# Switched attention: small matrix products in three groups per tile in place of six, routing later in the round

## The chip, the cores and the metric

One core of one Trainium2 chip. The core has five engines that run in parallel and meet at semaphores: TensorE (PE, with its weight loads as PEld), VectorE (DVE), ScalarE (ACT), GpSimd (POOL) and SyncE (SP, which here starts the transfers). The metric is the time of one execution on the device, in microseconds (us).

## The reference, cut to what matters

The whole is a model of four layers on x of 128 sequences x 64 positions x 128 features. Each layer adds a cross attention and a feed-forward part to x. The change touches the last part alone, the "switched attention" of layer 3:

```python
def _get_sel_gate(x, w, route_scale):              # per position and head: best 2 of 8 experts
    probs = jax.nn.sigmoid((x @ w.T).reshape(B, S, H, E))
    vals, idx = jax.lax.top_k(probs, K)
    vals = vals / jnp.clip(vals.sum(-1, keepdims=True), 1e-09) * route_scale
    return (jax.nn.one_hot(idx, E) * vals[..., None]).sum(-2)
...
x = layernorm(x)                                   # H = 8 heads, E = 8 experts, P = 128, K = 2
q = jnp.einsum('bsd,hpd->bhsp', x, q_w.reshape(H, P, D))
k = jnp.einsum('bsd,hpd->bhsp', x, k_w.reshape(H, P, D))
v = jnp.einsum('bshep,bshe->bhsp', jnp.einsum('bsd,hedp->bshep', x, v_w), gate_v)
att = jax.nn.softmax(jnp.einsum('bhqp,bhkp->bhqk', q, k) * P ** -0.5, axis=-1)
ctx = jnp.einsum('bhqk,bhkp->bqhp', att, v)
out = jnp.einsum('bshep,hepd->bsd', ctx[:, :, :, None, :] * gate_o[..., None], o_w)
```

All 64 experts are computed for every position, and the gates (zero for six of eight) weight their outputs. The result is added to the part's input, with the factor tanh(g_ffn[3]).

## The kernel before, in words

`program` runs the layers one after the other. The last two calls are the cross attention of layer 3, which leaves x in a scratch buffer in memory, and `switch_attention` (from L1687), which writes the output. Its helper `prepare_switch` (L1603) loads and splits the expert weights into a high and a low part, and keeps two small weights: `pair` (the product of query and key weights of each head, so that scores are x·pair·x) and `sel` (the routing weights of both gates).

**Tiles and rounds.** A tile is 128 rows of x (two sequences); there are 64. `straight` (L36) writes the program out: for every round t it goes through a list of stages (lag, step) and emits step for tile t - lag. Each engine has such a list of its own, and its order is the order of the code; semaphores tie them together. In round t the engines work on the v half of tile t - 2, the o half of tile t - 3, and the preparation of tile t - 1.

**Units.** The big work is 16 units a round, v0 to v7 (values of head 0 to 7) and o0 to o7 (outputs). A unit is six matmuls with 512 columns (L2062): three (high x high, high x low, low x high) into an accumulator bank `ps_a` for four experts, then three into a bank `ps_d` for the other four. There are two banks of each kind, used in turn, so bank d of a unit waits until the unit two before it has been read. ScalarE reads bank a (`scale`, L1850: four scalings by the gates), VectorE reads bank d (`mix`, L1964: four operations, each a gated product added to a partial sum, in two halves h0 and h1 of two). GpSimd adds the scaled parts: `add_v` (L1789, L1794) makes the values v, `add_o` (L1806 to L1816) and `finish` (L1823 to L1829) the output.

**Small products of TensorE, per round:** `turn_x` (L2070) transposes the normalised tile; `turns[0]` and `turns[1]` (L2077) transpose the softmax numerators; `logits` (L2082) is the routing product; `pair_keys(0)` and `(1)` (L2091) multiply by `pair`; `scores` (L2115); `context` (L2104) multiplies probabilities by v. Before the change these stand in six groups among the units: turn_x with turns[0] after v1; turns[1] with logits after v2; pair_keys(0) after v4; pair_keys(1) after v5; scores after o0; context after o1.

**VectorE's order.** The table `between` says what stands behind each half of each mix. `norm` (L244) is the first stage of the round: it normalises the tile that turn_x then transposes. `sums` (L1930 to L1934) makes gate_o. `route(n)` are the 20 steps of the top-2 routing of the next tile (L1973 to L1994), each waiting for the one before; step 0 waits for ScalarE's exponential of the logits, and step 19 writes gate_v, for which v0 of the next round waits on ScalarE and on VectorE. `peak` (L2016) takes the row maximum of the scores and `shifts` (L2022) scales and negates it; the exponentials of ScalarE use it as their bias. `low_ctx(b)` (L2010) makes the low part of the context. `front(n)` are the first three steps of the layer norm of a tile one round ahead (L217 to L223); GpSimd's `rstd` (L236), which stands between o5 and o6 in its list, needs front(2) and is needed by `norm`.

**ScalarE's order.** Scalings in unit order; keep_x (L1860, L1861) after v1, exp_logits (L1873) and keep_probs (L1867) after v3, keep_u after v5 and v6, keep_ctx and the exponentials (L1899) in the o half.

```python
def straight(stages, bufs=2, tiles=TILES):
    for t in range(tiles + max(lag for lag, _ in stages)):
        for lag, step in stages:
            if 0 <= t - lag < tiles:
                step(t - lag, (t - lag) % bufs, (t - lag) // bufs)
```

Of the kernel before, what the change touches and what calls it, by code (L numbers as in the profile page):

```python
# [1602 lines left out]
def prepare_switch(k, A, C):  # L1603
# [9 lines left out]
    with k.scope():  # L1613
# [8 lines left out]
        with nc.Block() as block:  # L1622
# [30 lines left out]
            @block.vector  # L1653
            def _(dve):
                dve.wait_ge(q["pair_ps"], 1)
                for n in range(2):
                    dve.tensor_copy(W["pair"][:, 4 * n:4 * n + 4], ps[n]).then_inc(q["kept"], 1)
                dve.wait_ge(q["sel_ps"], 1)
                dve.tensor_copy(W["sel"][:], ps_sel).then_inc(q["kept"], 1)
                ones = C["ones"][:, 0:SH]  # L1660
                dve.tensor_scalar(W["route"][:, 0], ones, rs[:], None, ALU.mult).then_inc(q["kept"], 1)
                dve.tensor_scalar(W["route"][:, 1], ones, rs[:], C["gates"][:, 7:8], ALU.mult, ALU.mult)\
                    .then_inc(q["kept"], 1)
                for h in range(SH):
                    for m, n in enumerate(("v", "o")):
                        dve.wait_ge(q["high"], 2 * h + m + 1)
                        dve.tensor_tensor(W[n]["low"][:, h], staged[:, h % 3, m], W[n]["high"][:, h].bitcast(F32),
                                          ALU.subtract)\
                            .then_inc(q["low"], 1)
# [17 lines left out]
def switch_attention(k, A, C, x_in, out):  # L1687
# [6 lines left out]
    with k.scope():  # L1694
# [9 lines left out]
        top = k.sb("sw_top", [P, SH])  # L1704
# [31 lines left out]
                   "ranked", "u", "uT", "scores", "top", "shift", "exp", "p_turned", "p_kept", "rsum",  # L1736
# [10 lines left out]
        with nc.Block() as block:  # L1747
# [87 lines left out]
            def _(act):  # L1835
# [58 lines left out]
                def exp_scores(i, s, rd, lo):  # L1894
                    act.wait_ge(q["shift"], i + 1)
                    if lo == 0 and not first(i, 2):
                        act.wait_ge(q["p_turned"], 2 * (i - 1))
                    for h in range(lo, lo + 2):
                        act.activation(probs[:, s, h], ps_s[:, h], ACT.Exp, bias=shift[:, s, h:h + 1],  # L1899
                                       scale=float(P) ** -0.5, accum_out=total[:, s, h:h + 1]).then_inc(q["exp"], 1)  # L1900
                exps = [(1, lambda i, s, rd, lo=lo: exp_scores(i, s, rd, lo)) for lo in range(0, SH, 2)]
                vs, os = ([(lag, scale(kind, h)) for h in range(SH)] for kind, lag in (("v", 2), ("o", 3)))
                stages = vs[:2] + [(1, keep_x)] + vs[2:4] + [(1, exp_logits), (2, keep_probs)] + vs[4:6]
# [5 lines left out]
            def _(dve):  # L1909
# [104 lines left out]
                def peak(i, s, rd):  # L2014
                    dve.wait_ge(q["scores"], i + 1)
                    dve.tensor_reduce(top[:], ps_s, AX.X, ALU.max).then_inc(q["top"], 1)  # L2016

                def shifts(i, s, rd):
                    dve.wait_ge(q["top"], i + 1)
                    if not first(i, 2):  # L2020
                        dve.wait_ge(q["exp"], SH * (i - 1))
                    dve.tensor_scalar(shift[:, s], top[:], -float(P) ** -0.5, None, ALU.mult).then_inc(q["shift"], 1)  # L2022

                mixes = {(kind, h): [(lag, mix(kind, h, half)) for half in range(2)]
                         for kind, lag in (("v", 2), ("o", 3)) for h in range(SH)}
# [3 lines left out]
                    "v": [[], [], [(2, sums(0))], [(2, sums(1))], [(2, sums(2))], [], *R[0:5], R[5] + R[6], R[7],  # L2029
                          R[8] + R[9], R[10], R[11]],  # L2030
                    "o": [R[12], R[13] + R[14], R[15] + R[16], [(1, peak)], [(1, shifts)], R[17], R[18],
                          [(2, low_ctx(0))], [(0, front(0))], R[19] + [(0, front(1))], [(0, front(2))],
                          [(2, low_ctx(1))], [], [], [], []],
# [8 lines left out]
            def _(pe):  # L2042
# [76 lines left out]
                stages = vs[:2] + [(1, turn_x), turns[0], vs[2], turns[1], (1, logits), vs[3], vs[4], (1, pair_keys(0))]  # L2119
                stages += [vs[5], (1, pair_keys(1)), vs[6], vs[7], os[0], (1, scores), os[1], (2, context)]  # L2120
# [52 lines left out]
```

## Time and profile before

| what | us |
|---|---|
| time, median of 3 runs | 3384.04 (3339.35 to 3385.38) |
| the profiled execution | 3386.34, its span 3384.6 |
| PE busy | 3020.6 (89%) |
| DVE busy | 2829.0 (84%) |
| ACT busy | 2356.9 (70%) |
| POOL busy | 2325.1 (69%) |
| first expert unit of the switched attention on TensorE | starts at 1467.54 |

The profile is of one execution. Each row of an engine's timeline has the start from the span's beginning, the duration, the engine, the line of the code, the operation, out<-in by the program's names, shapes, and xN where N equal ones in a row are merged (the duration then is from the first start to the last end). Operations of one engine overlap a little, since the next starts before the end of the one before is recorded; matmuls do so most, so for them the distance of two starts is the cost, not the duration. What stands in brackets is the engine's idle time before the row and who ended it. The view by stretches has the stretch, its length, then for PE, PEld, DVE, ACT and POOL the busy us and (xinstructions), the granted clock of TensorE (1.00 is full), the share of the DMA engines and GB/s.

### The profile page before, as it was taken

Reading aid. Unit: us, or ns where it says so; the run is one execution under the profiler, and the core shown is the slowest. Engines: PE = TensorE matmul, PEld = TensorE weight load, DVE = VectorE, ACT = ScalarE, POOL = GpSimd, SP = SyncE. Lnnn points to the kernel's source line nnn. Section 1 sums busy time; section 2 is a strip of 40 time slices with the busy share of each in tenths; the row PEclk is TensorE's granted clock in tenths of the full one; section 3 lists DMA queues with packets and bytes.
Section 4 is the critical chain, followed back from the end, with each engine's and each line's share of the span. In section 5 each row is a group of like instructions: output and inputs, shape, how many; then the busy total and the mean of one; then the engine's idle time right before and its main releaser. Section 6 shows DMA issues by size and latency. Waiting matters only on the chain.

```text
span 3384.6 us, 79947 instructions
## 1 busy us (share of the span) xinstructions
PE 3020.6 (89%) x24889; PEld 2212.5 (65%) x24902; DVE 2829.0 (84%) x9292; ACT 2356.9 (70%) x7581; POOL 2325.1 (69%) x3156
## 2 busy tenths in 40 slices
PE   6944999549865999679999999999999999999998
PEld 3522777427543677557777777777777777777776
DVE  4455999669897899678998899998899898889887
ACT  2345666678697666557777777777777777777776
POOL 1236999556487666237777777777777777777777
PEclk9999999759876999879999999999999999999999
DMA  1101000012100011310000000000000000000000
GB/s 53 55 8 18 16 16 16 3 40 79 43 1 7 27 31 30 89 48 9 8 8 8 7 8 8 9 8 8 7 8 8 8 9 7 9 7 8 9 8 5
DMA packets 134373, 63.81 MB, mean 19 GB/s; under 512 B 21824, under 2 KB 133568, under 8 KB 133952
## 3 DMA queue, kind: packets, MB, share of 16 engines
q1 hardware_dynamic: 133952, 58.70, 6.3%
q8 instruction: 202, 3.31, 0.4%
q14 instruction: 219, 1.79, 0.2%
HBM read 41.81 MB, written 8.45 MB: 15 GB/s over the span
## 4 chain that ended last, share of the span: by engine, by line
PE 56%; POOL 0%; DVE 0%; ACT 0%; issue 0%; DMA 0%; POOLq 0%; SPq 0%; DVEq 0%; ACTq 0%
PE ps_sw_a L2062 23%; PE ps_sw_d L2062 21%; PE ps_sw_w L2104 4%; PE ps_sw_w L2091 3%; PE ps_sw_s L2077 2%; PE ps_sw_s L2115 2%; PE ps_sw_m L2082 1%; PE ps_sw_m L2070 0%; ACT sw_scaled L1850 0%; DVE sw_v_part L1964 0%; POOL sw_o_rest L1813 0%; POOL sw_o_rest L1816 0%; DMA sw_x<-scratch_x 0%; POOL sw_o_rest L1809 0%; POOL sw_o_pair L1825 0%
## 5 line engine op out<-in xcount | busy, mean ns | idle before, releaser
L1850 ACT ACTIVATE sw_scaled<-ps_sw_a,sw_gate_o 128x128 f32<-128x128 f32 x2048 | 620.3, 447 | 252.3 <-PE ps_sw_a L2062 244.2
L1850 ACT ACTIVATE sw_scaled<-ps_sw_a,sw_gate_v 128x128 f32<-128x128 f32 x2048 | 597.4, 450 | 203.3 <-PE ps_sw_a L2062 203.2
L1964 DVE SCALAR_TENSOR_TENSOR sw_o_part<-ps_sw_d,sw_gate_o,sw_o_part 128x128 f32<-128x128 f32 x1920 | 554.7, 337 | 60.4 <-PE ps_sw_d L2062 59.4
L1789 POOL TENSOR_TENSOR sw_v_pair<-sw_v_part,sw_scaled 128x256 f32<-128x256 f32 x512 | 377.9, 738 | 159.1 <-DVE sw_v_part L1964 105.5
L1964 DVE SCALAR_TENSOR_TENSOR sw_v_part<-ps_sw_d,sw_gate_v,sw_scaled 128x128 f32<-128x128 f32 x1024 | 304.6, 338 | 124.2 <-PE ps_sw_d L2062 102.7
L1813 POOL TENSOR_TENSOR sw_o_rest<-sw_o_rest,sw_scaled 128x256 f32<-128x256 f32 x384 | 285.2, 743 | 154.6 <-ACT sw_scaled L1850 117.3
L1964 DVE SCALAR_TENSOR_TENSOR sw_v_part<-ps_sw_d,sw_gate_v,sw_v_part 128x128 f32<-128x128 f32 x1024 | 304.3, 338 | 0.0
L1816 POOL TENSOR_TENSOR sw_o_rest<-sw_o_rest,sw_scaled 128x256 f32<-128x256 f32 x384 | 282.6, 736 | 30.1
L1794 POOL TENSOR_TENSOR sw_v<-sw_v_pair 128x128 f32<-128x128 f32 x512 | 241.6, 472 | 40.2
L920 POOL TENSOR_TENSOR at_key_wide<-at_keyT,c_half_heads 128x1024 f32<-128x1024 f32 x128 | 242.5, 1895 | 4.2 <-ACT at_keyT L1017 4.2
L2062 PE MATMUL ps_sw_a<-sw_v_high,sw_xT_high 128*128 128x512 f32 x512 | 235.8, 461 | 0.0
L2062 PE MATMUL ps_sw_a<-sw_o_high,sw_ctx_high 128*128 128x512 f32 x512 | 214.7, 419 | 0.6 <-ACT sw_scaled L1850 0.6
L2062 PE MATMUL ps_sw_d<-sw_v_high,sw_xT_high 128*128 128x512 f32 x512 | 208.2, 407 | 0.0
L2062 PE MATMUL ps_sw_d<-sw_o_high,sw_ctx_high 128*128 128x512 f32 x512 | 207.1, 404 | 0.0
L2062 PE MATMUL ps_sw_d<-sw_v_low,sw_xT_high 128*128 128x512 f32 x512 | 203.2, 397 | 0.0
L2062 PE MATMUL ps_sw_a<-sw_v_low,sw_xT_high 128*128 128x512 f32 x512 | 202.9, 396 | 0.0
L2062 PE MATMUL ps_sw_a<-sw_v_high,sw_xT_low 128*128 128x512 f32 x512 | 202.5, 395 | 0.0
L2062 PE MATMUL ps_sw_a<-sw_o_low,sw_ctx_high 128*128 128x512 f32 x512 | 202.0, 395 | 0.0
L2062 PE MATMUL ps_sw_d<-sw_v_high,sw_xT_low 128*128 128x512 f32 x512 | 202.0, 395 | 0.0
L2062 PE MATMUL ps_sw_d<-sw_o_low,sw_ctx_high 128*128 128x512 f32 x512 | 201.4, 393 | 0.0
L2062 PE MATMUL ps_sw_a<-sw_o_high,sw_ctx_low 128*128 128x512 f32 x512 | 200.4, 391 | 0.0
L2062 PE MATMUL ps_sw_d<-sw_o_high,sw_ctx_low 128*128 128x512 f32 x512 | 200.4, 391 | 0.0
(318 smaller groups left out, 8768.4 us busy)
## 6 DMA issues: line engine op xcount, KB each, us to landing
at_ctxT<-ctx_T SPq DMA_DIRECT2D x128, 64.0 KB, 1.8
re_values<-in_ctx SPq DMA_DIRECT2D x128, 64.0 KB, 2.3
x<-in_x SPq DMA_DIRECT2D x64, 64.0 KB, 1.8
l_ctx<-in_ctx SPq DMA_DIRECT2D x64, 64.0 KB, 2.0
re_ctx<-in_ctx SPq DMA_DIRECT2D x16, 256.0 KB, 3.3
scratch_x<-x SPq DMA_DIRECT2D x64, 64.0 KB, 1.8
swp_staged<-in_L_ffn_v_w SPq DMA_DIRECT2D x8, 512.0 KB, 5.6
swp_staged<-in_L_ffn_o_w SPq DMA_DIRECT2D x8, 512.0 KB, 6.9
```

Source lines behind the costliest of these rows:

```text
L920: pool.tensor_tensor(key_wide[:, s], keyT[:, s].unsqueeze(1).broadcast_to([P, HALF, P]), C["half_heads"][:].unsqueeze(2).broadcast_to([P, ...
L1789: pool.tensor_tensor(v_pair[:, h % 2], v_part[:, h], scaled[:, h % 4, 2:4], ALU.add)\
L1794: pool.tensor_tensor(v[:, h], v_pair[:, h % 2, 0], v_pair[:, h % 2, 1], ALU.add).then_inc(q["v"], 1)
L1813: pool.tensor_tensor(o_rest[:, 0:2], o_rest[:, 0:2], scaled[:, h % 4, 0:2], ALU.add)\
L1816: pool.tensor_tensor(o_rest[:, 2:4], o_rest[:, 2:4], scaled[:, h % 4, 2:4], ALU.add)\
L1850: act.activation(scaled[:, h % 4, e], ps_a[h % 2][:, e], ACT.Copy, scale=gates[:, s, h, HALF_E + e:HALF_E + e + 1]).then_inc(a_scaled[kind ...
L1964: dve.scalar_tensor_tensor(out=acc[:, e % 2], in0=ps_d[h % 2][:, e], scalar=gates[:, s, h, e:e + 1], in1=before, op0=ALU.mult, op1=ALU.add ...
L2062: m = pe.matmul(bank, lhs[a], w[b][:, h, experts], start=c == 0, stop=c == 2)
L2077: m = pe.matmul(ps_s[t, h], probs[t, s, h], C["ident"][t, t], start=True, stop=True)
L2091: m = pe.matmul(ps_w[n][:, h * P:(h + 1) * P], W["pair"][:, 4 * n + h], xT[:, s], start=True, stop=True)
L2104: m = pe.matmul(ps_w[b][:, h * S:(h + 1) * S], v[t, h], probs_T[t, h], start=True, stop=True)
L2115: m = pe.matmul(ps_s[t], xT[:, s, t], uT[:, :, t], start=True, stop=True)
```

## The change

TensorE's small products stand in three groups: turn_x with both turns after v1; logits with both pair_keys after v4; scores with context after o1. VectorE's routing starts after the first half of v5 (before: of v3) and its 20 steps run to the end of the round; peak stands behind the first half of o2 (before: the second half of o1); front(0) to front(2) stand between o4 and o6. ScalarE's keep_probs stands behind v2 and its exp_logits behind v4. The factor P ** -0.5 goes into the weights `pair`, so that the scores come scaled; the reduction of peak writes its result negated, and shifts, its buffer and its semaphore are gone.

```diff
@@ prepare_switch, VectorE @@
                 for n in range(2):
-                    dve.tensor_copy(W["pair"][:, 4 * n:4 * n + 4], ps[n]).then_inc(q["kept"], 1)
+                    dve.tensor_scalar(W["pair"][:, 4 * n:4 * n + 4], ps[n], float(P) ** -0.5, None, ALU.mult).then_inc(q["kept"], 1)
@@ switch_attention @@
-        top = k.sb("sw_top", [P, SH])
         shift = k.sb("sw_shift", [P, 2, SH])
...
-                   "ranked", "u", "uT", "scores", "top", "shift", "exp", "p_turned", "p_kept", "rsum",
+                   "ranked", "u", "uT", "scores", "shift", "exp", "p_turned", "p_kept", "rsum",
@@ ScalarE @@
                         act.activation(probs[:, s, h], ps_s[:, h], ACT.Exp, bias=shift[:, s, h:h + 1],
-                                       scale=float(P) ** -0.5, accum_out=total[:, s, h:h + 1]).then_inc(q["exp"], 1)
+                                       accum_out=total[:, s, h:h + 1]).then_inc(q["exp"], 1)
...
-                stages = vs[:2] + [(1, keep_x)] + vs[2:4] + [(1, exp_logits), (2, keep_probs)] + vs[4:6]
+                stages = vs[:2] + [(1, keep_x), vs[2], (2, keep_probs)] + vs[3:5] + [(1, exp_logits), vs[5]]
@@ VectorE @@
                 def peak(i, s, rd):
                     dve.wait_ge(q["scores"], i + 1)
-                    dve.tensor_reduce(top[:], ps_s, AX.X, ALU.max).then_inc(q["top"], 1)
-
-                def shifts(i, s, rd):
-                    dve.wait_ge(q["top"], i + 1)
                     if not first(i, 2):
                         dve.wait_ge(q["exp"], SH * (i - 1))
-                    dve.tensor_scalar(shift[:, s], top[:], -float(P) ** -0.5, None, ALU.mult).then_inc(q["shift"], 1)
+                    dve.tensor_reduce(shift[:, s], ps_s, AX.X, ALU.max, negate=True).then_inc(q["shift"], 1)
...
-                    "v": [[], [], [(2, sums(0))], [(2, sums(1))], [(2, sums(2))], [], *R[0:5], R[5] + R[6], R[7],
-                          R[8] + R[9], R[10], R[11]],
-                    "o": [R[12], R[13] + R[14], R[15] + R[16], [(1, peak)], [(1, shifts)], R[17], R[18],
-                          [(2, low_ctx(0))], [(0, front(0))], R[19] + [(0, front(1))], [(0, front(2))],
-                          [(2, low_ctx(1))], [], [], [], []],
+                    "v": [[], [], [(2, sums(0))], [(2, sums(1))], [(2, sums(2))], [], [], [], [], [], R[0], R[1], R[2], R[3],
+                          R[4], R[5]],
+                    "o": [R[6], R[7], R[8], R[9], [(1, peak)], R[10] + R[11], R[12], [(2, low_ctx(0))], R[13],
+                          R[14] + [(0, front(0))], R[15] + [(0, front(1))], [(2, low_ctx(1))], R[16] + [(0, front(2))],
+                          R[17], R[18], R[19]],
@@ TensorE @@
-                stages = vs[:2] + [(1, turn_x), turns[0], vs[2], turns[1], (1, logits), vs[3], vs[4], (1, pair_keys(0))]
-                stages += [vs[5], (1, pair_keys(1)), vs[6], vs[7], os[0], (1, scores), os[1], (2, context)]
+                stages = vs[:2] + [(1, turn_x)] + turns + vs[2:5] + [(1, logits), (1, pair_keys(0)), (1, pair_keys(1))]
+                stages += vs[5:] + os[:2] + [(1, scores), (2, context)]
                 stages += os[2:]
```

## Rows read from the trace of the kernel before

**Rows 1.** The view by stretches, 600 us of the steady stage (columns: see above)

```profile
2300.00:2900.00 600.00, 600.00 (x3702) 456.99 (x3702) 540.25 (x1914) 455.15 (x1774) 457.57 (x709) 1.00 0.03 8
```

**Rows 2.** VectorE in order of time, one round: start us, us, engine, what [idle before]

```profile
2502.87 2.14 DVE L1964 SCALAR_TENSOR_TENSOR sw_o_part<-ps_sw_d,sw_gate_o,sw_o_part 128x128 f32<-128x128 f32 x8
2504.94 0.79 DVE L244 TENSOR_SCALAR sw_xhat<-sw_x,sw_mv,sw_rstd 128x128 f32<-128x128 f32 x1
...
2508.87 0.61 DVE L1964 SCALAR_TENSOR_TENSOR sw_v_part<-ps_sw_d,sw_gate_v,sw_scaled 128x128 f32<-128x128 f32 x2 [0.60 <-PE ps_sw_d L2062]
...
2511.30 0.61 DVE L1964 SCALAR_TENSOR_TENSOR sw_v_part<-ps_sw_d,sw_gate_v,sw_scaled 128x128 f32<-128x128 f32 x2 [0.88 <-PE ps_sw_d L2062]
...
2514.31 0.59 DVE L1964 SCALAR_TENSOR_TENSOR sw_v_part<-ps_sw_d,sw_gate_v,sw_v_part 128x128 f32<-128x128 f32 x2
...
2520.18 0.28 DVE L1984 TENSOR_TENSOR sw_r_w<-sw_r_eq,sw_place 128x128 f32<-128x128 f32 x1
...
2524.61 0.68 DVE L2016 TENSOR_REDUCE sw_top<-ps_sw_s 128x8 f32<-128x512 f32 x1
2526.16 0.61 DVE L1964 SCALAR_TENSOR_TENSOR sw_o_part<-ps_sw_d,sw_gate_o,sw_o_part 128x128 f32<-128x128 f32 x2 [0.87 <-PE ps_sw_d L2062]
2526.68 0.16 DVE L2022 TENSOR_SCALAR sw_shift<-sw_top 128x8 f32<-128x8 f32 x1
...
2534.70 0.79 DVE L244 TENSOR_SCALAR sw_xhat<-sw_x,sw_mv,sw_rstd 128x128 f32<-128x128 f32 x1
```

**Rows 3.** TensorE in order of time, the same round

```profile
2506.33 0.27 PE L2070 MATMUL ps_sw_m<-c_ident,sw_xhat 128*128 128x128 f32 x1
...
2508.41 0.40 PE L2062 MATMUL ps_sw_d<-sw_v_high,sw_xT_low 128*128 128x512 f32 x1
2508.74 0.68 PE L2077 MATMUL ps_sw_s<-c_ident,sw_probs 64*64 64x64 f32 x16
...
2509.60 0.48 PE L2062 MATMUL ps_sw_a<-sw_v_high,sw_xT_high 128*128 128x512 f32 x1
2509.92 0.39 PE L2062 MATMUL ps_sw_a<-sw_v_low,sw_xT_high 128*128 128x512 f32 x1
...
2512.25 0.40 PE L2062 MATMUL ps_sw_d<-sw_v_high,sw_xT_low 128*128 128x512 f32 x1
2512.48 1.05 PE L2091 MATMUL ps_sw_w<-sw_xT,sw_pair 128*128 128x128 f32 x8
...
2515.58 0.48 PE L2062 MATMUL ps_sw_a<-sw_v_high,sw_xT_high 128*128 128x512 f32 x1
...
2519.15 0.39 PE L2062 MATMUL ps_sw_d<-sw_o_high,sw_ctx_high 128*128 128x512 f32 x1
...
2519.61 0.39 PE L2062 MATMUL ps_sw_d<-sw_o_high,sw_ctx_low 128*128 128x512 f32 x1
2519.93 1.08 PE L2115 MATMUL ps_sw_s<-sw_uT,sw_xT 128*64 128x512 f32 x4
...
2522.53 2.00 PE L2104 MATMUL ps_sw_w<-sw_probs_T,sw_v 64*128 64x64 f32 x32
```

**Rows 4.** ScalarE and GpSimd in order of time, the same round

```profile
2508.15 1.14 ACT L1850 ACTIVATE sw_scaled<-ps_sw_a,sw_gate_v 128x128 f32<-128x128 f32 x4 [0.39 <-PE ps_sw_a L2062]
...
2516.59 0.74 POOL L1789 TENSOR_TENSOR sw_v_pair<-sw_v_part,sw_scaled 128x256 f32<-128x256 f32 x1 [0.27 <-DVE sw_v_part L1964]
...
2521.94 0.46 POOL L1794 TENSOR_TENSOR sw_v<-sw_v_pair 128x128 f32<-128x128 f32 x1
```

**Rows 5.** All engines in order of time, the first round

```profile
1459.33 0.35 DVE L244 TENSOR_SCALAR sw_xhat<-sw_x,sw_mv,sw_rstd 128x128 f32<-128x128 f32 x1 [0.66 <-POOL sw_rstd L236]
...
1459.73 0.47 PE L2070 MATMUL ps_sw_m<-c_ident,sw_xhat 128*128 128x128 f32 x1 [33.63 <-DVE sw_xhat L244]
```

**Rows 6.** The tile sw_r_sel: how often, ns shortest/median/longest, first and last start

```profile
L1979 DVE TENSOR_TENSOR sw_r_sel<-sw_r_w,sw_m_w x54: 797/806/812, 1713.6 to 3289.4; 128x128 f32<-128x128 f32 x54
...
L1986 DVE TENSOR_TENSOR sw_r_sel<-sw_r_w,sw_m_w x54: 386/401/406, 1718.6 to 3294.4; 128x128 f32<-128x128 f32 x54
```

## The prediction

> **What bounds the kernel now.** I read the page's slices first: from about 1,460 us to the end the kernel is in the switched attention, TensorE near full in each slice. The view by stretches makes it exact [rows 1]: in 600 us of the steady stage TensorE is busy for all 600, VectorE for 540, ScalarE for 455, GpSimd for 458, at a granted clock of 1.00 (the 2.4 GHz level). So TensorE sets the pace and VectorE, at 90%, is the next. Two normalised tiles, one round apart, start at 2504.94 and 2534.70 on VectorE [rows 2]: a round is 29.76 us, and there are 64 tiles.
>
> Second, TensorE in order of time [rows 3]. A matmul of a unit (six with 512 columns, bank a and then bank d) starts 0.23 us after the one before (2519.15 to 2519.61 are two steps). Around the small products it is longer. After a group, the first matmul of the unit holds its successor back for 0.32 (2509.60 to 2509.92): 0.09 for leaving a group. Entering costs 0.10 ahead of the turned probabilities (2508.41 to 2508.74 is 0.33 against 0.23), 0.09 ahead of the scores (2519.61 to 2519.93), and nothing ahead of the paired keys (2512.25 to 2512.48). That is the whole gain to be had from fewer groups.
>
> Third, VectorE in the same round [rows 2]. It waits for TensorE at v2 (0.60), v3 (0.88) and o2 (0.87); from o2 at 2526.16 it runs without a gap until it starts the next tile's normalisation at 2534.70. TensorE needs the result of that for its first small product, turn_x. So there is a second loop beside TensorE's own: turn_x at 2506.33 [rows 3], TensorE's work up to VectorE's start on o2 (19.83 us), VectorE's unbroken stretch (8.54), the normalisation (0.79). That is 29.16 of the 29.76 us. The loop through VectorE has 0.60 us to spare, and this is the number on which the change turns.
>
> **The change part by part.** *Grouping.* The three exits that go are worth 3 x 0.09 = 0.27; the entry of the second turn_probs goes too, 0.10. Logits now enter from a unit, 128x128 as the paired keys are, so at nothing. Context now follows scores: I give 0 of its 0.09 entry back, since its tile shape (64*128) differs from that of the scores (128*64), and keep 0.09 as the upper end. Sum 0.37 us per round, bounds 0.27 to 0.46. Lengths of the products stay.
>
> On that 0.09 the Trainium skill speaks, in TensorEngine Tiling (Array Packing), Key Properties: changing the tiling mode drains TensorE. The rows agree in that only the groups that begin with 64-row or 64-column tiles pay to enter [rows 3]; by the rule scores to context pays on, and without it a round would be 0.09 shorter.
>
> *VectorE's order.* The work sum hardly changes: shifts goes (0.16 us busy, about 0.08 of its time as the next starts 0.08 before its end), negating in the reduction I take at nothing (bounds 0 and the 0.08 it saves) [rows 2]. What changes is where it stands. Routing starts after v5 in place of v3, because the logits now come behind v4. Before, steps 10 to 16 and the peak stood ahead of o2: from step 10 at 2520.18 to the start of the peak at 2524.61, plus its 0.60 (0.68 less the 0.08), is 5.03 us [rows 2]. In it stand ten mixes of 0.26 (eight run 2.14 with a last overlap of 0.08, so 2.06/8), 2.60. The rest, 2.43, is now behind the gate of o2. Less the 0.08 of shifts, the unbroken stretch grows by 2.35 us: 8.54 to 10.89. Nothing in the stretch goes elsewhere; step 17 to 19, both low_ctx and the three front steps were in it already. The time freed lies ahead of v5 and is idle there: VectorE is done with v4 before v5 is made, and with routing not begun it has nothing to do.
>
> *A new wait at o0.* Bank d of o0 needs the mixes of v6. VectorE's chain v5, step 0, v5, step 1, v6, step 2, v6 is as long as v3 to v4 was: 2511.30 to 2514.31 and 0.60 for the last pair, 3.61 us, and it starts 0.46 behind v5's last matmul (as 2508.41 and 2508.87 show for v2): done at 4.07. TensorE, with both paired keys already behind it, wants the bank 0.23 + (2519.15 - 2515.58 - 0.09) = 3.71 us after that matmul [rows 2, 3]. It waits 0.36, with the signal 0.38; bounds 0 and 0.5 (o1 has the same with v7, nearly hidden). Queued behind it are o0, o1, scores and context, and so the gate of o2.
>
> *Context and GpSimd.* Context stood at 2522.53, 0.13 behind the end of GpSimd's last v sum at 2522.40 [rows 3, 4]. Its TensorE time moves up by 0.37, which the 0.38 at o0 returns, so I take 0; bounds 0 and 0.2.
>
> *Handover to turn_x.* It was hidden: its weights were loaded under the unit before. Now TensorE waits for the normalisation, as in the first round, where it took 0.05 from 1459.68 (1459.33 and 0.35) to the start, and the transpose had 0.47 in place of 0.27 [rows 5]. I take 0.25, bounds 0.05 and 0.3. Also queued behind the normalisation: the gates of step 19, for which ScalarE's first v scaling waits. Step 19 ends 0.79 + 0.25 ahead of turn_x's start and four scalings take 1.14 [rows 4], so v0's bank is free 0.1 into the small products, and v2 asks for it only behind turn_x and both turn_probs: covered.
>
> *The port of VectorE and GpSimd.* The same comparison takes 0.81 at one place (L1979) and 0.40 at another (L1986), over 54 rounds each [rows 6]. At 2516.59 GpSimd had just begun a sum of 0.74 [rows 4], between v5 and v6 where the slow one stands. Normalising takes 0.79, against 0.35 in the first round, when GpSimd was idle. Moving routing among GpSimd's o sums can add such waits (up to +0.5 for steps 10 and 12 to 15), and GpSimd's new wait for front(2), now after o6, can take some away (xhat at 0.35: -0.44). I take 0.
>
> In the skill, SBUF — State Buffer, Who interferes with whom, says that an instruction of VectorE with two SBUF inputs is blocked by a GpSimd one that reads SBUF until that ends. By that rule steps 10 to 14 all stand at risk in the o half, and the round would be up to the 0.5 longer that I keep as an end.
>
> *Rest.* ScalarE's keep_probs moves ahead of the logits' exponential; both have several us before their readers. ScalarE has 24% idle [rows 1]. The scaled pair weights are two instructions in the preparation. GpSimd's o6 and o7 come later by its wait for front(2), but stay about as far from turn_x. SP's transfers keep their waits. All at 0.
>
> **Sum.** Loop after: (19.83 - 0.37) + 0.38 + 10.89 + 0.79 + 0.25 = 31.77 us, against 29.76: +2.01 us per round. Handovers with an o half before them: 61 of the 64. 61 x 2.01 = +123 us. The profiled execution took 3386.34 (span 3384.6), 2.3 above the median of 3384.04; 3384 + 123 = 3507 us.
>
> **Rivals.** (1) *The VectorE loop does not bind*, the round stays TensorE's: -0.37 x 64 = -24, so 3360 us, not slower. For it: the gain itself is in the rows. Against: it needs a VectorE loop under 29.39, 2.4 us less than I add up; it decides from a stretch after o2 of 8.5 us, and 2.35 us of work were put there. Chance 0.13. A faster result over 2% (under 3316) would need a gain of over 1 us per round, which no row offers: 0.04.
> (2) *Half as bad*: normalising unblocked (-0.44), no wait at o0 (-0.38), handover 0.05 (-0.2): +1.0 per round, 3445 us, within 2%. For it: GpSimd then stands still while it waits for front(2). Chance 0.11.
> (3) *Worse*: port waits +0.5 and o0, o1 and context at their upper ends (+0.3): 2.01 + 0.8 = +2.8 per round, 3384 + 61 x 2.8 = 3555 us. For it: GpSimd is busy in 76% of the time [rows 1]. Against: the eight mixes of the row at 2502.87 keep their 0.26 each all the same [rows 2], so only the routing steps are open to it. Chance 0.14.
> My forecast has the remaining 0.58.
>
> **Numbers.** 2% is 68 us, about what a measurement of this kernel can tell from no change, or 1.1 us per round. Slower 0.78 (forecast, rival 3 and about half of rival 2), same 0.18, faster 0.04. The range runs from rival 2's side, 3435, to 3565; rival 1 and a little are left out.
>
> **What would show it.** The profile after should have: a round of 31.8 us between two normalisations; VectorE never waiting for TensorE between o2 and the normalisation, that stretch near 10.9; TensorE idle or with late starts at bank d of o6, o7, v0, v1, and at turn_x, released by VectorE (some 2.4 us per round); VectorE idle over 2 us ahead of v5; three exits from small groups per round. If turn_x does not wait for the normalisation, the forecast is wrong at its root. If it does and the round is not 31 to 32.5, a term (port, o0, handover) is mis-sized.

## Result and the profile after

The changed kernel takes 3456.86 us (median of 6 runs, 3454.93 to 3457.21) against 3384.68 (6 runs). The ratio is 1.0249 with a 95% interval of 1.0191 to 1.0307: slower by 72 us, where 123 were predicted. That it is slower is clear; whether by more than 2% is not, since the interval reaches below. The profiled execution spans 3455.2 us. One thing is needed to read the medians and intervals: single executions of some versions, two of the six of the kernel before among them (3339.35 and 3340.9), are 43 to 51 us shorter, and in the one profile of such an execution (the first experiment below) the difference lies ahead of the switched attention, whose first normalised tile stands at 1411.1 us there and at 1461.2 in the changed kernel.

The stretches of the steady stage first (columns as in rows 1), of the changed kernel:

```profile
2300.00:2900.00 600.00, 587.74 (x3548) 437.60 (x3547) 489.46 (x1826) 441.67 (x1706) 448.54 (x685) 1.00 0.03 8
```

TensorE is no longer busy throughout, and VectorE fell further, from 540 to 489 us of 600. No engine is full: the time is in a chain that goes back and forth between two of them. VectorE in order of time, one round of the changed kernel:

```profile
2522.31 0.61 DVE L1963 SCALAR_TENSOR_TENSOR sw_v_part<-ps_sw_d,sw_gate_v,sw_scaled 128x128 f32<-128x128 f32 x2 [2.28 <-PE ps_sw_d L2057]
...
2532.72 0.61 DVE L1963 SCALAR_TENSOR_TENSOR sw_o_part<-ps_sw_d,sw_gate_o,sw_o_part 128x128 f32<-128x128 f32 x2 [2.23 <-PE ps_sw_d L2057]
2533.24 0.68 DVE L2017 TENSOR_REDUCE sw_shift<-ps_sw_s 128x8 f32<-128x512 f32 x1
...
2541.11 0.60 DVE L1963 SCALAR_TENSOR_TENSOR sw_o_part<-ps_sw_d,sw_gate_o,sw_o_part 128x128 f32<-128x128 f32 x2
...
2543.34 0.34 DVE L244 TENSOR_SCALAR sw_xhat<-sw_x,sw_mv,sw_rstd 128x128 f32<-128x128 f32 x1
...
2553.19 0.61 DVE L1963 SCALAR_TENSOR_TENSOR sw_v_part<-ps_sw_d,sw_gate_v,sw_scaled 128x128 f32<-128x128 f32 x2 [2.28 <-PE ps_sw_d L2057]
```

From v5 (2522.31) to the next v5 (2553.19) the round is 30.88 us; before, it was 29.76 [rows 2]. VectorE stands idle for 2.28 us ahead of v5 and for 2.23 ahead of o2, where it had 0.87, and then runs from o2 to the normalisation in 10.62 us (2532.72 to 2543.34), where it took 8.54. 61 rounds x 1.12 = 68 of the 72 us. The reduction that now negates (2533.24) takes 0.68 as the plain one did.

TensorE in the same round, around bank d of o0, o5 and v0, and at turn_x:

```profile
2525.35 0.40 PE L2057 MATMUL ps_sw_a<-sw_o_high,sw_ctx_low 128*128 128x512 f32 x1
2525.62 0.50 PE L2057 MATMUL ps_sw_d<-sw_o_high,sw_ctx_high 128*128 128x512 f32 x1
2525.96 0.40 PE L2057 MATMUL ps_sw_d<-sw_o_low,sw_ctx_high 128*128 128x512 f32 x1
...
2535.79 0.39 PE L2057 MATMUL ps_sw_a<-sw_o_high,sw_ctx_low 128*128 128x512 f32 x1
2536.56 0.51 PE L2057 MATMUL ps_sw_d<-sw_o_high,sw_ctx_high 128*128 128x512 f32 x1 [0.38 <-DVE sw_o_part L1963]
...
2541.26 0.40 PE L2057 MATMUL ps_sw_a<-sw_v_high,sw_xT_low 128*128 128x512 f32 x1
2541.76 0.51 PE L2057 MATMUL ps_sw_d<-sw_v_high,sw_xT_high 128*128 128x512 f32 x1
...
2543.74 0.39 PE L2057 MATMUL ps_sw_d<-sw_v_high,sw_xT_low 128*128 128x512 f32 x1
2543.97 0.27 PE L2065 MATMUL ps_sw_m<-c_ident,sw_xhat 128*128 128x128 f32 x1
```

A step of 0.23 is free of waits. At bank d of o5 it is 0.77 (2535.79 to 2536.56), of o6 0.56, of o7 0.33, of v0 0.50; of o0 0.27 and of o1 0.29, and a first matmul behind such a wait holds its successor back for 0.34 (2525.62 to 2525.96), so 0.11 more. Turn_x does not wait: 2543.74 to 2543.97 is 0.23, and the normalisation had ended at 2543.68. The waits view of 1,700 to 3,300 us (us in total, times, longest) names both sides of the chain, and a third party:

```profile
PEld ps_sw_d L2057 <- DVE sw_o_part L1963: 127.3, 250, 0.8
DVE sw_o_part L1963 <- PE ps_sw_d L2057: 113.8, 51, 2.3
POOL sw_rstd L236 <- DVE sw_var L223: 60.4, 52, 1.2
```

### The profile page after: what moved, and what is told of

It is laid out like the page before. It is cut to its first block, busy times and chain, and to the rows that moved or that the text cites. A ratio compares the mean times of both kernels' runs of the same rounds, so it can differ in the third digit from the quotient of the medians.

```text
span 3455.2 us, 79883 instructions
## 1 busy us (share of the span) xinstructions
PE 3046.0 (88%) x24889; PEld 2200.7 (64%) x24902; DVE 2730.4 (79%) x9228; ACT 2368.7 (69%) x7581; POOL 2347.9 (68%) x3156
## 4 chain that ended last, share of the span: by engine, by line
PE 40%; DVE 15%; issue 2%; POOL 0%; ACT 0%; DMA 0%; POOLq 0%; SPq 0%; DVEq 0%; ACTq 0%
PE ps_sw_d L2057 15%; PE ps_sw_a L2057 14%; DVE sw_o_part L1963 8%; PE ps_sw_w L2099 4%; PE ps_sw_w L2086 3%; DVE sw_ctx_low L2009 2%; PE ps_sw_s L2072 2%; PE ps_sw_s L2110 2%; DVE sw_shift L2017 1%; DVE sw_r_w L1983 1%; DVE sw_chosen L1987 1%; PE ps_sw_m L2077 0%; DVE sw_stats L217 0%; DVE sw_r_sel L1986 0%; DVE sw_r_sel L1985 0%
## 5 line engine op out<-in xcount | busy, mean ns | idle before, releaser
L1849 ACT ACTIVATE sw_scaled<-ps_sw_a,sw_gate_o 128x128 f32<-128x128 f32 x2048 | 602.5, 406 | 255.9 <-PE ps_sw_a L2057 250.8
L1849 ACT ACTIVATE sw_scaled<-ps_sw_a,sw_gate_v 128x128 f32<-128x128 f32 x2048 | 586.8, 393 | 261.1 <-PE ps_sw_a L2057 251.7
L1963 DVE SCALAR_TENSOR_TENSOR sw_o_part<-ps_sw_d,sw_gate_o,sw_o_part 128x128 f32<-128x128 f32 x1920 | 568.4, 338 | 145.0 <-PE ps_sw_d L2057 144.9
L1812 POOL TENSOR_TENSOR sw_o_rest<-sw_o_rest,sw_scaled 128x256 f32<-128x256 f32 x384 | 286.5, 746 | 219.8 <-ACT sw_scaled L1849 182.5
L1815 POOL TENSOR_TENSOR sw_o_rest<-sw_o_rest,sw_scaled 128x256 f32<-128x256 f32 x384 | 296.2, 771 | 30.1
L2057 PE MATMUL ps_sw_d<-sw_o_high,sw_ctx_high 128*128 128x512 f32 x512 | 234.7, 458 | 33.5 <-DVE sw_o_part L1963 33.3
L2057 PE MATMUL ps_sw_a<-sw_v_high,sw_xT_high 128*128 128x512 f32 x512 | 215.3, 420 | 0.0
```

The costliest lines, as they stand in the source:

```text
L1812: pool.tensor_tensor(o_rest[:, 0:2], o_rest[:, 0:2], scaled[:, h % 4, 0:2], ALU.add)\
L1815: pool.tensor_tensor(o_rest[:, 2:4], o_rest[:, 2:4], scaled[:, h % 4, 2:4], ALU.add)\
L1849: act.activation(scaled[:, h % 4, e], ps_a[h % 2][:, e], ACT.Copy, scale=gates[:, s, h, HALF_E + e:HALF_E + e + 1]).then_inc(a_scaled[kind ...
L1963: dve.scalar_tensor_tensor(out=acc[:, e % 2], in0=ps_d[h % 2][:, e], scalar=gates[:, s, h, e:e + 1], in1=before, op0=ALU.mult, op1=ALU.add ...
L2057: m = pe.matmul(bank, lhs[a], w[b][:, h, experts], start=c == 0, stop=c == 2)
```

## Experiments

Theory: a loop through VectorE sets the round, made of TensorE's work from turn_x to o2 and VectorE's unbroken stretch from o2 on. Rivals: the new groups on TensorE cost the time; VectorE's total work does; another engine takes over.

### The groups undone, the late routing kept

```diff
-                stages = vs[:2] + [(1, turn_x)] + turns + vs[2:5] + [(1, logits), (1, pair_keys(0)), (1, pair_keys(1))]
-                stages += vs[5:] + os[:2] + [(1, scores), (2, context)]
+                stages = vs[:2] + [(1, turn_x), turns[0], vs[2], turns[1], (1, logits), vs[3], vs[4], (1, pair_keys(0))]
+                stages += [vs[5], (1, pair_keys(1)), vs[6], vs[7], os[0], (1, scores), os[1], (2, context)]
```

ScalarE's list went back to the order before as well.

> The changed kernel, with TensorE's and ScalarE's lists as they were before (six groups); VectorE's late routing stays. Theory (the loop through VectorE sets the round: TensorE from turn_x to o2, then VectorE's unbroken stretch): the stretch stays at 10.6 us, TensorE's part is 0.37 longer for the grouping and 0.3 shorter since it need not wait at o0 and o1, so the round stays at 30.9 to 31.1 us and the time at 3455 to 3470 us. Rival (the new groups on TensorE cost the time, for instance since ScalarE and VectorE get their inputs in bunches): it goes back to 3384 us or near it.

Measured: four executions, 3423.25, 3426.89, 3470.0 and 3471.06 us, median 3448.45, ratio 1.0177 (1.0112 to 1.0242). The first two have the head start described above, so it is the other two that stand against the changed kernel's 3457: 13 to 14 us longer, at the upper end of what was expected. The rounds of its profile settle the matter. Two normalised tiles in a row, VectorE:

```profile
2503.36 0.34 DVE L244 TENSOR_SCALAR sw_xhat<-sw_x,sw_mv,sw_rstd 128x128 f32<-128x128 f32 x1
...
2534.48 0.34 DVE L244 TENSOR_SCALAR sw_xhat<-sw_x,sw_mv,sw_rstd 128x128 f32<-128x128 f32 x1
```

A round of 31.12 us, 0.24 longer than with three groups. The groups are not what costs; they save a little, and late routing costs by itself. The 0.24 is what the later experiments leave to expect: 0.55 for the grouping, less the 0.32 for the late starts at o0 and o1, which are absent here.

### Part of the routing back ahead of o2

The three groups stay. Steps 10 to 12, or 10 to 16, are put behind o1, in VectorE's idle time ahead of o2:

```diff
-                    "o": [R[6], R[7], R[8], R[9], [(1, peak)], R[10] + R[11], R[12], ...
+                    "o": [R[6], R[7], R[8], R[9] + R[10] + R[11] + R[12], [(1, peak)], [], [], ...
```

> The changed kernel with only steps 10 to 12 put ahead of the wait for o2. They take 1.03 us of the stretch. Theory (each us taken from the stretch is a us of the round until TensorE's own loop binds): 62 x 1.0 us less, 3395 us, a round of 29.9 us. Rival (another engine takes over at once, so that there is no slope of one): a gain of under half of that, 3425 us or more.

> The changed kernel with routing steps 10 to 16 put behind o1, ahead of the wait for o2; all groups stay three. In the changed profile these steps take 1.6 us of the stretch behind o2, and VectorE stands idle for 2.23 us ahead of o2. Theory: they disappear into the idle time, the loop through VectorE falls to 29.25 us, TensorE's own loop of 29.4 to 29.7 takes over, and the time is 3360 to 3382 us: not over the kernel before. Rival (groups cost the time): it stays at 3457 us. Rival (VectorE's total work bounds): stays within 10 us of 3457.

Measured: 3394.64 us (3393.27 to 3394.99) with steps 10 to 12, and 3376.64 (3375.01 to 3377.74, ratio to the kernel before 0.9967, 0.9952 to 0.9982) with 10 to 16. Both fell where they were expected. The first is a slope of one: 1.03 us taken from the stretch, 62 us off the time. VectorE of the version with steps 10 to 12, from one normalised tile to the next:

```profile
2508.22 0.34 DVE L244 TENSOR_SCALAR sw_xhat<-sw_x,sw_mv,sw_rstd 128x128 f32<-128x128 f32 x1
...
2528.46 0.61 DVE L1963 SCALAR_TENSOR_TENSOR sw_o_part<-ps_sw_d,sw_gate_o,sw_o_part 128x128 f32<-128x128 f32 x2 [1.27 <-PE ps_sw_d L2057]
...
2538.07 0.34 DVE L244 TENSOR_SCALAR sw_xhat<-sw_x,sw_mv,sw_rstd 128x128 f32<-128x128 f32 x1
```

The round is 29.85 us, the idle time ahead of o2 has shrunk from 2.23 to 1.27 us, and the stretch from o2 is 9.61. With steps 10 to 16 moved the idle time ahead of o2 is 0.20, and TensorE is nearly full again:

```profile
2300.00:2900.00 600.00, 599.08 (x3697) 458.92 (x3695) 523.22 (x1907) 458.57 (x1781) 461.47 (x710) 1.00 0.03 8
```

The gain levels off there: some 0.6 us more taken from the stretch give 18 us more, half of what a slope of one would give.

### The fold alone

The kernel before, with only the factor in the pair weights, the negated reduction and no shifts.

```diff
-                    dve.tensor_reduce(top[:], ps_s, AX.X, ALU.max).then_inc(q["top"], 1)
...
-                    dve.tensor_scalar(shift[:, s], top[:], -float(P) ** -0.5, None, ALU.mult).then_inc(q["shift"], 1)
+                    dve.tensor_reduce(shift[:, s], ps_s, AX.X, ALU.max, negate=True).then_inc(q["shift"], 1)
```

> The kernel before with one part of the change alone: the factor in the pair weights, the peak negated in its reduction, no shifts. Theory: 0.08 us per round less on VectorE, in a stretch that has 0.6 us to spare: 3384 us, within 4. Rival (the negating reduction or the exponential without a scale costs or saves time on the path): over 6 us either way. The reduction should take 0.68 us as before.

Measured: 3384.92 us (3343.28 to 3389.81) beside 3386.00, ratio 0.9965 (0.991 to 1.0019). No difference that these runs can tell.

### The same work added in two places

Three reductions of a constant tile per round on VectorE, once ahead of v5 and once behind step 11:

```diff
+                def pad(i, s, rd):
+                    for n in range(3):
+                        if n or not first(i, 1):
+                            dve.wait_ge(q["spare"], 3 * i + n)
+                        dve.tensor_reduce(spare[:], place[:], AX.X, ALU.max).then_inc(q["spare"], 1)
...
-                    "v": [[], [], [(2, sums(0))], [(2, sums(1))], [(2, sums(2))], [], [], [], [], [], R[0], ...
+                    "v": [[], [], [(2, sums(0))], [(2, sums(1))], [(2, sums(2))], [], [], [], [], [(1, pad)], R[0], ...
```

In the other version the table of v stays and R[10] + R[11] becomes R[10] + R[11] + [(1, pad)].

> The changed kernel with three added reductions on VectorE per round (0.27 us each and 0.04 between, about 0.85 us in all, of a constant tile, so no product reads them), in its idle 2.28 us ahead of v5. Theory (only the stretch behind o2 counts): the time stays at 3457 us, within 5. Rival (VectorE's total work binds): the same gain as with the reductions in the stretch, some 50 us more.

> The same three reductions behind routing step 11, in the unbroken stretch from o2 to the normalisation. Theory: each of the 61 rounds is 0.85 us longer: +52 us, 3509 us (3500 to 3515). Rival (a loop that closes elsewhere): under half of that.

Measured: 3453.32 us (3452.21 to 3455.88) and 3504.09 us (3501.29 to 3507.14). The same work, 0.92 us with a last overlap of 0.08, is free in the one place and costs 47 us (against the changed kernel) to 51 us (against the other version) in the other, where 52 were expected. VectorE with it ahead of v5:

```profile
2515.70 0.92 DVE L2024 TENSOR_REDUCE sw_spare<-sw_place 128x16 f32<-128x128 f32 x3
2518.07 0.61 DVE L1964 SCALAR_TENSOR_TENSOR sw_v_part<-ps_sw_d,sw_gate_v,sw_scaled 128x128 f32<-128x128 f32 x2 [1.45 <-PE ps_sw_d L2064]
```

and with it behind step 11, two normalised tiles in a row, 31.70 us apart:

```profile
2505.70 0.33 DVE L244 TENSOR_SCALAR sw_xhat<-sw_x,sw_mv,sw_rstd 128x128 f32<-128x128 f32 x1
...
2537.40 0.33 DVE L244 TENSOR_SCALAR sw_xhat<-sw_x,sw_mv,sw_rstd 128x128 f32<-128x128 f32 x1
```

In the first the idle time ahead of v5 is 1.45 in place of 2.28, and the round is 30.85 us (normalised tiles at 2508.23 and 2539.08), as in the changed kernel. Total work of VectorE is refuted as the bound.

### Steps 0 and 1 moved into the idle time

```diff
-                    "v": [..., [], R[0], R[1], R[2], R[3], R[4], R[5]],
+                    "v": [..., R[0] + R[1], [], [], R[2], R[3], R[4], R[5]],
```

> The changed kernel with only routing steps 0 and 1 moved, from behind v5's two halves to behind v4, in the idle time. The stretch behind o2 is as it was. Theory: TensorE's late starts at bank d of o0 and o1 (0.15 and 0.17 us with the restart) go, 0.3 us per round: 3438 us (3435 to 3444). Rival (they were hidden by something else, so only the stretch counts): 3457 us.

Measured: 3436.49 us (median of 10, 3390.25 to 3445.7), 20 us less than the changed kernel, as the two waits had been added up; in its profile TensorE's late starts at o0 and o1 are gone. Its round is 30.56 us by the normalised tiles at 2504.23 and 2534.79.

### What the grouping is worth

Two versions in which VectorE has little to do, so that TensorE sets the round; they differ from each other only in TensorE's and ScalarE's lists, by the diff of the first experiment. Both leave out routing steps 3 to 13, the choice of the two best experts, so that nine steps are left of 20 and the result is not the model's:

```diff
-RANK = 20
+RANK = 9
...
-                            lambda: dve.tensor_tensor(chosen[:, s], r["p"][:], r["sel"][:], ALU.mult),
-                            lambda: dve.tensor_tensor(rm["sum"][:], rm["m1"][:], rm["m2"][:], ALU.add),
+                            lambda: dve.tensor_tensor(chosen[:, s], r["p"][:], r["p"][:], ALU.mult),
+                            lambda: dve.tensor_tensor(rm["sum"][:], rm["m1"][:], rm["m1"][:], ALU.add),
...
-                    "v": [..., [], R[0], R[1], R[2], R[3], R[4], R[5]],
+                    "v": [..., R[0] + R[1], R[2], R[3], R[4], R[5], R[6], R[7]],
```

> Leaves out routing steps 3 to 13 (the choice of the two best experts; all are weighted by their squared sigmoid) so that VectorE does not bind, with TensorE's and ScalarE's lists in six groups. Only for its difference from its pair with three groups, which has the same VectorE list. Theory: TensorE sets the round, 29.4 to 29.7 us, without the small late starts at the end of the o half; 3360 to 3380 us.

> The same work left out as in its pair (routing steps 3 to 13), with three groups on TensorE. Theory: the prediction's term for the grouping, 0.37 us per round with bounds 0.27 and 0.46: 24 us less than the pair (17 to 30). Rival (a group's entry and exit cost nothing where TensorE is otherwise fed, the gaps being overlapped): less than 10 us between the two.

Measured: 3386.97 us (10 runs, 3384.54 to 3395.08) with six groups, 3351.77 (4 runs, 3350.21 to 3353.45) with three: 35.2 us, 0.55 per tile, where 0.37 was predicted and 0.46 was the upper end. Two expectations missed: the difference was to be 17 to 30 us, and the version of six 3360 to 3380 us. That one is no faster than the kernel before (3386.22 beside it, ratio 1.0006, 0.9996 to 1.0015), although eleven of VectorE's routing steps are gone: the kernel before was bound by TensorE. TensorE in order of time, six groups:

```profile
2506.50 0.68 PE L2057 MATMUL ps_sw_s<-c_ident,sw_probs 64*64 64x64 f32 x16
2507.11 0.50 PE L2042 MATMUL ps_sw_a<-sw_v_high,sw_xT_high 128*128 128x512 f32 x1
...
2512.43 1.05 PE L2071 MATMUL ps_sw_w<-sw_xT,sw_pair 128*128 128x128 f32 x8
2513.24 0.48 PE L2042 MATMUL ps_sw_a<-sw_v_high,sw_xT_high 128*128 128x512 f32 x1
...
2519.93 1.08 PE L2095 MATMUL ps_sw_s<-sw_uT,sw_xT 128*64 128x512 f32 x4
2520.93 0.50 PE L2042 MATMUL ps_sw_a<-sw_o_high,sw_ctx_high 128*128 128x512 f32 x1
```

and three:

```profile
2515.62 1.15 PE L2057 MATMUL ps_sw_s<-c_ident,sw_probs 64*64 64x64 f32 x32
2516.70 0.50 PE L2042 MATMUL ps_sw_a<-sw_v_high,sw_xT_high 128*128 128x512 f32 x1
...
2521.22 1.95 PE L2071 MATMUL ps_sw_w<-sw_xT,sw_pair 128*128 128x128 f32 x16
2522.93 0.48 PE L2042 MATMUL ps_sw_a<-sw_v_high,sw_xT_high 128*128 128x512 f32 x1
...
2530.11 1.08 PE L2095 MATMUL ps_sw_s<-sw_uT,sw_xT 128*64 128x512 f32 x4
2531.12 2.00 PE L2084 MATMUL ps_sw_w<-sw_probs_T,sw_v 64*128 64x64 f32 x32
2533.05 0.50 PE L2042 MATMUL ps_sw_a<-sw_o_high,sw_ctx_high 128*128 128x512 f32 x1
```

In the version of three the distance from scores to context is 1.01 us and that from scores to the next unit, with six groups, 1.00: context costs no more behind scores than a unit does there, and the 0.09 that it pays behind a unit is saved. That is the 0.09 that I had kept as an upper end only. Both transposes of the probabilities in a row take 1.08 us, where one alone takes 0.61 to the next row: 0.14 less than twice. Both paired keys in a row go the other way: 1.71 us to the next row, where one alone takes 0.81: 0.09 more than twice.

### The gaps filled

```diff
+                    "v": [..., R[0] + R[1] + R[2] + R[3], R[4], R[5], R[6], R[7], R[8], R[9]],
+                    "o": [R[10], R[11], R[12], R[13] + R[14] + R[15] + R[16], [(1, peak)], R[17], R[18], [(2, low_ctx(0))], [], [(0, front(0))], [(0, front(1))], [(2, low_ctx(1))], [(0, front(2))], R[19], [], []],
```

A second version has steps 17 to 19 and all three front steps behind step 16 too.

> The changed kernel with routing steps 0 to 3 put behind v4, in VectorE's idle 2.28 us ahead of v5, and the others moved up so that steps 10 to 16 stand ahead of the wait for o2. All work is done. Theory: the waits at o0 and o1 go as well (v6's mixes are earlier), TensorE's own loop sets the round at 29.1 to 29.4 us: 3345 to 3362 us, under the kernel before and under the version with only steps 10 to 16 moved (3377). Rival (the o0 and o1 waits did not cost anything, or another engine binds at 29.5): 3370 to 3380 us.

> As the version with steps 0 to 3 behind v4, and steps 17 to 19 and the three front steps ahead of the wait for o2 too. Theory: VectorE then has more slack behind o2 than TensorE can use, and the time is that of the other within 5 us. Rival (VectorE's loop still binds there): 10 us or more below it. Rival (too much work ahead of o2, so that its mixes are late): above it.

Measured: 3352.64 us (3350.71 to 3355.67; ratio to the kernel before 0.9905, 0.989 to 0.992) and 3355.23 us (3352.93 to 3358.93; 0.9913, 0.9898 to 0.9927). Both beat the kernel before, by about 1%, and the changed one, and both fell where they were expected. The first stands where the version without half the routing stands (3351.77), so VectorE has gone from the path. VectorE's wait at o2 in it:

```profile
2504.26 0.61 DVE L1963 SCALAR_TENSOR_TENSOR sw_o_part<-ps_sw_d,sw_gate_o,sw_o_part 128x128 f32<-128x128 f32 x2 [1.48 <-PE ps_sw_d L2054]
2512.88 0.73 DVE L244 TENSOR_SCALAR sw_xhat<-sw_x,sw_mv,sw_rstd 128x128 f32<-128x128 f32 x1
```

The stretch from o2 to the normalisation is 8.62 us, against 8.54 before the change and 10.62 after it.

### The front steps earlier

```diff
-                          [(2, low_ctx(0))], R[13], R[14] + [(0, front(0))], R[15] + [(0, front(1))], [(2, low_ctx(1))], R[16] + [(0, front(2))],
+                          [(2, low_ctx(0))], R[13] + [(0, front(0))], R[14] + [(0, front(1))], R[15] + [(0, front(2))], [(2, low_ctx(1))], R[16],
```

Only front(2) moves by two places; front(0) and front(1) move by one.

> The changed kernel with the three front steps two places earlier (behind o4 and the first half of o5), so that GpSimd no longer stands 1.16 us in front of its rstd and its o sums 6 and 7 come earlier. The work of the stretch is the same. Theory (the normalisation took 0.34 us in place of the predicted 0.79 because GpSimd is pushed away from it by that wait): it is back at 0.5 to 0.8 us, turn_x waits for it, and the time is 5 to 25 us more than 3457. Rival (its length has to do with the negated peak or the place in the round, not with GpSimd): 0.34 us and 3457 us.

Measured: 3484.11 us (3482.03 to 3492.49), 27 us more, for the same work; but the normalisation stayed at 0.33 to 0.35 us in every round. The expectation of the time was just missed, and its reason fell: turn_x does not wait for the normalisation here either. VectorE and GpSimd in order of time in this version, ahead of the normalised tile:

```profile
2523.96 0.73 POOL L1812 TENSOR_TENSOR sw_o_rest<-sw_o_rest,sw_scaled 128x256 f32<-128x256 f32 x1
...
2524.34 0.39 DVE L1989 TENSOR_SCALAR sw_m_clip<-sw_m_sum 128x16 f32<-128x16 f32 x1
...
2525.64 0.74 POOL L1812 TENSOR_TENSOR sw_o_rest<-sw_o_rest,sw_scaled 128x256 f32<-128x256 f32 x1
2525.75 0.66 DVE L1991 TENSOR_TENSOR sw_norm<-sw_m_inv,sw_route 128x16 f32<-128x16 f32 x1
...
2526.86 0.42 DVE L1993 TENSOR_TENSOR sw_gate_v<-sw_chosen,sw_norm 128x64 f32<-128x64 f32 x1
2527.20 0.33 DVE L244 TENSOR_SCALAR sw_xhat<-sw_x,sw_mv,sw_rstd 128x128 f32<-128x128 f32 x1
```

and in the changed kernel:

```profile
2540.97 0.17 DVE L1989 TENSOR_SCALAR sw_m_clip<-sw_m_sum 128x16 f32<-128x16 f32 x1
...
2542.22 0.33 DVE L1991 TENSOR_TENSOR sw_norm<-sw_m_inv,sw_route 128x16 f32<-128x16 f32 x1
...
2542.60 0.74 POOL L1815 TENSOR_TENSOR sw_o_rest<-sw_o_rest,sw_scaled 128x256 f32<-128x256 f32 x1
...
2543.00 0.42 DVE L1993 TENSOR_TENSOR sw_gate_v<-sw_chosen,sw_norm 128x64 f32<-128x64 f32 x1
...
2543.48 0.79 POOL L1812 TENSOR_TENSOR sw_o_rest<-sw_o_rest,sw_scaled 128x256 f32<-128x256 f32 x1
```

The clip at 2524.34 falls into GpSimd's sum of 2523.96 to 2524.69, ends 0.04 behind it and takes 0.39, against 0.17 (2540.97) where GpSimd stood waiting. The product into sw_norm at 2525.75 starts behind the sum of 2525.64 and takes 0.66, against 0.33. These 0.22 and 0.33 account for the 0.50 us by which this stretch is longer (11.12, from 2516.08 to 2527.20, against 10.62). Step 19 (gate_v, 2526.86, and 2543.00 in the changed kernel) outlasts a sum of GpSimd, takes 0.42, and the normalisation starts in the gap before GpSimd's next. In the kernel before, GpSimd was first, by 0.04 us:

```profile
2534.66 0.74 POOL L1816 TENSOR_TENSOR sw_o_rest<-sw_o_rest,sw_scaled 128x256 f32<-128x256 f32 x1
```

The normalisation of 2534.70 [rows 2] came behind it and took 0.79. In the changed kernel it is GpSimd's sum that comes second (2543.48) and takes 0.79 in place of 0.74. So the length of the normalisation does not depend on whether GpSimd waits for front(2); that wait does keep other instructions short. It depends on where the normalisation falls between GpSimd's sums. What stands ahead of it on VectorE is one way to shift it, but not the only one: in the light version of six groups the mixes of o7 stand ahead of it as in the kernel before, and it takes 0.33 all the same, begun 0.06 before a sum ends:

```profile
2533.81 0.74 POOL L1812 TENSOR_TENSOR sw_o_rest<-sw_o_rest,sw_scaled 128x256 f32<-128x256 f32 x1
2534.49 0.33 DVE L244 TENSOR_SCALAR sw_xhat<-sw_x,sw_mv,sw_rstd 128x128 f32<-128x128 f32 x1
```

This is read from the order of the rows; no run changed that order alone.

## Why the prediction was right, and where a link and its sizes were off

The direction and the range held (3435 to 3565), and so did the main mechanism, a loop through VectorE whose stretch behind o2 sets the round. The size was 123 us for 72, and one link of the mechanism was wrong: the prediction said that turn_x would wait for the normalisation and called itself wrong at its root if it did not. It does not. That the range held owes something to its width of 130 us: 3457 lies nearer to rival 2 (3445, chance 0.11) than to the forecast (3507). The steps:

- **The loop through VectorE takes over from TensorE's.** Right. The waits of both sides are in the profile; adding work in the stretch, taking work from it and adding it elsewhere gave slopes of about one, one and zero.
- **Routing behind the gate of o2, +2.35 us.** The term that carries the change; the stretch grew by 2.08 (8.54 to 10.62). It was mis-sized by 0.27, because moved instructions do not keep the lengths that they had beside GpSimd's work. This goes both ways: step 10 took 0.28 us by its median before and 0.59 after. The largest change is that of step 15, the sum of the two maxima, with 0.55 us by its median of 50 before and 0.16 after:

```profile
L1989 DVE TENSOR_TENSOR sw_m_sum<-sw_m_m x50: 164/546/574, 1720.5 to 3177.4; 128x16 f32<-128x16 f32 x50
```

```profile
L1988 DVE TENSOR_TENSOR sw_m_sum<-sw_m_m x49: 154/160/165, 1705.5 to 3187.6; 128x16 f32<-128x16 f32 x49
```

- **Grouping, -0.37 us.** Failed in size: the pair of light versions gives -0.55. Their rows give -0.51: the 0.37, 0.09 for context and 0.14 for the transposes, less 0.09 for the paired keys. I denied context its 0.09 because its tile shape differs from that of scores. The Trainium skill says in TensorEngine Tiling (Array Packing), Key Properties, that a change of tiling mode drains TensorE. The rows neither refute this nor show a drain: the step from the second half of scores to context is 0.53 (2528.55 to 2529.08 in the changed kernel), 0.05 longer than that between the halves of scores (2528.07 to 2528.55), and the step from scores to a unit is 0.53 too (2520.41 to 2520.94 in the kernel before). What fell is only my reading that context would go on paying its 0.09. The lengths of the products, which I had said would stay, changed in both directions, and I had not looked for that.
- **The new wait at o0, +0.38 us.** About right in sum, not in place: 0.04 + 0.11 at o0 and 0.06 + 0.11 at o1, which I had called nearly hidden, make 0.32, and moving two steps away returned 20 us, 0.33 per round.
- **Context and GpSimd at nothing.** Right: context starts 1.01 behind scores, with no wait.
- **TensorE from turn_x to o2: 19.84 us predicted.** 19.83 - 0.51 + 0.32 = 19.64; in the profile 2532.72 less the 2513.10 of turn_x (2543.97 less the round's 30.87) is 19.62.
- **Normalisation 0.79 and handover 0.25, 1.04 us.** This step failed, in the length and in the wait: 0.63 from the start of the normalisation to turn_x (2543.34 to 2543.97), a miss of 0.41 and the largest. It took 0.34, ended 0.29 before TensorE asked for it, and turn_x's weights were loaded in time. 
- **Where the loop closes.** Ahead of the normalisation, through the banks d: the mixes of o6 end at 2541.71 and v0 starts its bank at 2541.76. By that path the round is 19.62 from turn_x to o2, 8.99 from o2 to the end of the mixes of o6, 0.05 and 2.21 from v0's bank d to turn_x, 30.87 us. Work behind the mixes of o6 is off it, with about 0.2 us to spare by an estimate from the rows (the mixes of o7 end at 2543.08, and v1 starts its bank at 2543.27). Where the last experiment has 0.33 more there (the product into sw_norm), TensorE starts v1's bank d 0.20 late and still does not wait at turn_x. No run changed that place alone; the padded and moved steps of the experiments on the slope stood ahead of the end of the mixes of o6, where both ways of closing the loop give the same. I had that path in the list of late starts, but took the normalisation for the one that ends last. The late starts stand at o5, o6, o7 and v0, not at o6, o7, v0 and v1, and make 0.54 + 0.33 + 0.10 + 0.27 over the step of 0.23, and 0.11 behind each: 1.68 us, where I expected 2.4 with turn_x. Rival 2 had the short normalisation and the short handover, but its reason, that GpSimd stands still while it waits for front(2), fell with the last experiment.
- **The sum:** 19.62 + 10.62 + 0.63 = 30.87 us against 31.77. The measured terms are distances along one round and add up in any case, so this sum sizes the misses and does not show where the loop closes. The three misses (0.22, 0.27, 0.41) have one sign, so none hid another.
- **The port.** I took 0, with both ends open; it was 0.27 less in the stretch and 0.45 less for the normalisation. The Trainium skill's SBUF — State Buffer, Who interferes with whom, says of a VectorE instruction in a two-port mode that whoever issues first holds the shared pair for the whole instruction and the other is blocked. Whether the normalisation runs in such a mode no run here shows. The trace agrees on the order: 0.79 for a normalisation begun 0.04 us behind GpSimd, 0.34 for one begun 0.14 us ahead of it. It does not show a whole block: the long one ends 0.09 behind GpSimd's sum (2534.66 and 0.74), not its own 0.34 behind, and GpSimd's sum that comes second is 0.05 longer, though 0.20 of the normalisation was left. Of the steps 10 to 14, which I had all called at risk by that rule, only step 10 grew by over 0.02 us, and step 11, a reduction with one input, did not belong among them.
- **Negation and scale at nothing.** Right as far as can be told: the reduction takes 0.68 as before, and the fold alone shows no difference beyond its interval.
- **VectorE idle over 2 us ahead of v5, and released by TensorE.** Right (2.28).

## What to carry to other kernels

When an engine with 10% to spare hands work back and forth with a full one, add up the loop (the one's work up to the gate, then the other's unbroken stretch behind it) and not the busy shares: here 0.60 us of slack stood against 2.1 us moved behind the gate, and the kernel with the emptier VectorE was the slower. Follow each hand-over to the one that really ends last: here it is a bank given back, not the normalised tile that looks like the natural end. The change's idea was good for 35 us on TensorE, and it needed only that the displaced work be put into the idle time that the new order opens (behind v4, ahead of o2), not spread evenly over the round.

## What the runs showed of the hardware that was not expected

- Two sets of 64*64 transposes in a row took TensorE 1.08 us, against 0.61 for one by itself, and two sets of 128*128 products 1.71, against 0.81. Going on from products with 128*64 weights to such with 64*128 took 1.01 us from start to start, and to a unit 1.00, while going to either from a unit's 128*128 costs 0.09.
- A matmul that starts late because its bank was not free holds the next one back for 0.34 us in place of 0.23, so that each wait costs 0.11 us more than its length.
- The same normalisation takes 0.34 us where it begins in the gap before GpSimd's next sum and 0.79 where it begins 0.04 us behind that sum's start. In the changed kernel VectorE's instruction ahead of it ends with GpSimd's sum and so leaves it the gap.
